# Graph attention kernel: the score vectors of the last two layers made in three column groups of TensorE's array

## The chip, the cores and the metric

The kernel runs on one core of one Trainium2 chip. The core has four engines that compute, each with its own instruction stream: TensorE (PE in the profile; its weight loads are listed as PEld), VectorE (DVE), ScalarE (ACT) and GpSimd (POOL). SyncE (SP) issues most DMAs here. The metric is the device time of one execution in microseconds (us), where lower is better.

## What is computed

The input is a graph of 1250 nodes with 768 features and 40000 edges of three types. There are four attention layers: two without relations (4 heads of 192, 2 heads of 96), then two with three relations (4 heads of 192, 1 head of 768). The part that the change touches is how the last two layers get their attention scores:

```python
def rgat_conv(x, W, q, k, b, src, dst, etype, heads, out_ch, n_nodes):
    xr = jnp.einsum('nd,rdf->rnf', x, W)        # W: 3 relations x 768 x 768
    oi = xr[etype, dst]
    oj = xr[etype, src]
    qi = oi @ q                                 # q, k: 768 x heads
    kj = oj @ k
    alpha = jax.nn.leaky_relu(qi + kj, NEG_SLOPE)
    m = jax.ops.segment_max(alpha, dst, num_segments=n_nodes)
    e = jnp.exp(alpha - m[dst])
    z = jax.ops.segment_sum(e, dst, num_segments=n_nodes)
    a = e / (z[dst] + EPS)
    msg = (a[:, :, None] * oj.reshape(-1, heads, out_ch)).reshape(-1, heads * out_ch)
    out = jax.ops.segment_sum(msg, dst, num_segments=n_nodes)
    return out + b
```

A node's score is x @ (W[r] @ q). So the kernel makes the small products W[r] @ q and W[r] @ k once, the score vectors: for each relation 768 numbers per head for q and as many for k. They depend on the weights alone, and are made early, long before the layer that uses them.

## The kernel before

The program is one hand-written instruction stream per engine, tied together by semaphores. The order on each engine is that of the code. Phases end with a barrier of all engines (`end_phase`). The first phase (0 to some 395 us) counts the edges into dense matrices, projects the first layer, and then has the mask stage, from 285 to 390 us of the span. Everything that the change moves is there.

The mask stage makes 40 masks (10 tiles of nodes x 4), each of which says where a row of the graph has no edge:

- DVE writes mask n in bf16 (`no_edges`, line 1683, into a ring of 3, so it waits until mask n-3 has been turned).
- PE turns it with 10 transposes (line 925) into PSUM bank 3 or 5; it waits for the mask (`nm_ready`) and until ACT has copied mask n-2 (`nm_copied`).
- ACT copies the turned mask to SBUF (line 1268, a ring of 6), and SP writes it to HBM (line 528, 320 KB).
- DVE, after every four masks, reads one of the turned masks four times, once for each head of the first layer (`tensor_tensor_reduce`, line 1697), to find the largest score of each node. Its results, the last of which ends the stage, give `pq`, which PE turns (line 935), ACT copies (line 1280) and SP sends through HBM. The first layer's attention waits for that.

Between the masks PE makes the score vectors. The weights come transposed in 12 halves (2 layers x 3 relations x 2 halves of 384 columns), each 1152 KB, into a ring of 3 in SBUF; POOL issues the load of half i when `score_rows` i-3 is done (line 722). After the masks 2, 5, 8 and so on PE runs `score_columns(i - 1)` and then `score_rows(i)`:

- `score_rows(i)` (line 902): six float32 matmuls, one for each 128 rows of the inner dimension f, added up in PSUM bank 7. The stationary operand is `qk1[:, f, :]` (8 columns: q and k of 4 heads) or `qk2[:, f, :]` (2 columns), the moving one is 128 x 384 of the weights. In the trace each float32 matmul is two rows, each with its own weight load.
- ACT copies the 8 or 2 result rows to `v_rows` (line 1259).
- `score_columns(i)` (line 910): three transposes of 128 columns each turn these rows into columns in bank 0; at the end ACT saves them in `vtab` (line 1278).

`cols` is a small table of constants, loaded by one DMA at the start, that holds `qk1` in its columns 24 to 71 and `qk2` in 72 to 83.

Of the kernel before, what the change touches and what calls it, by code (L numbers as in the profile page):

```python
# [20 lines left out]
F32 = mybir.dt.float32  # L21
# [4 lines left out]
ALU = mybir.AluOpType  # L26
ACT = mybir.ActivationFunctionType
AX = mybir.AxisListType

P = 128  # L30
N = 1250
D = 768
# [3 lines left out]
DT = D // P  # L36
# [67 lines left out]
C = Conv("c", [0, 1, 2], 4, 192, 384, 8, 4, 1, True, 1)  # L104
# [29 lines left out]
def gnn_program(nc, t_in, out):  # L134
    with ExitStack() as ctx:
        def sb(name, shape, dt):
            return ctx.enter_context(nc.sbuf_tensor(name, shape, dt))
# [21 lines left out]
        identf = sb("identf", [P, P], F32)  # L159
# [14 lines left out]
        epsc = sb("epsc", [P, 1], F32)  # L174
        winoff = sb("winoff", [P, NW], F32)
        tab = sb("tab", [1, 192], I32)
        cols = sb("cols", [P, 84], F32)
        scale2 = sb("scale2", [2, 1], F32)
        sconst = sb("sconst", [P, 4], F32)

        ps = ctx.enter_context(nc.psum_tensor("ps", [P, 8 * 512], F32))

        def bank(b, n=512, at=0):
            return ps[:, b * 512 + at:b * 512 + at + n]
# [16 lines left out]
        al2 = cols[0:96, 20:24].rearrange("p (j c) -> p j c", j=2)  # L201
        qk1 = cols[:, 24:72].rearrange("p (j c) -> p j c", j=DT)
        qk2 = cols[:, 72:84].rearrange("p (j c) -> p j c", j=DT)

# [45 lines left out]
        wt_half = [carve(work, i % 3 * WTH, WTH).rearrange("p (f d) -> p f d", f=DT) for i in range(12)]  # L252
        WT_HALVES = [(c, r, h) for c in (C, DD) for r in range(RELS) for h in range(2)]
# [3 lines left out]
        def v_cols(i, j):  # L257

            c, r, h = WT_HALVES[i]
            n2 = 2 * c.heads  # L260
            return (0 if c is C else RELS * DT * 8) + (r * DT + h * (DT // 2) + j) * n2
# [480 lines left out]
        def _(pe):  # L742
# [151 lines left out]
            def score_rows(i):  # L894

                c, r, h = WT_HALVES[i]
                pe.wait_ge(wt_in[i % 3], 16 * (i // 3 + 1))
                if i:
                    pe.wait_ge(v_copied, i)
                qk = qk1 if c is C else qk2  # L900
                for f in range(DT):
                    last = mm(ps[0:2 * c.heads, 7 * 512:7 * 512 + D // 2], qk[:, f, :], wt_half[i][:, f, :],
                              start=(f == 0), stop=(f == DT - 1))
                last.then_inc(v_done, 1)

            def score_columns(i):
                n2 = 2 * WT_HALVES[i][0].heads
                pe.wait_ge(v_copied, i + 1)
                for j in range(DT // 2):
                    last = nc.tensor.transpose(bank(0, n2, v_cols(i, j)),  # L910
                                               v_rows[i % 2][0:n2, j * P:(j + 1) * P], identf[0:n2, 0:n2])
                last.then_inc(v_turned, 1)


# [224 lines left out]
        def _(act):  # L1139
# [112 lines left out]
            nc.scalar.activation(s02[:, :, 0:A.RH], sd[:, :, 0:A.RH], ACT.Copy, scale=0.2)  # L1252

            def copy_v_rows(i):
                n2 = 2 * WT_HALVES[i][0].heads
                act.wait_ge(v_done, i + 1)
                if i >= 2:
                    act.wait_ge(v_turned, i - 1)
                nc.scalar.activation(v_rows[i % 2][0:n2, :], ps[0:n2, 7 * 512:7 * 512 + D // 2], ACT.Copy).then_inc(v_copied, 1)

            for n, (r, t) in enumerate(MASKS):
                act.wait_ge(nm_turned, n + 1)
# [251 lines left out]
        def _(dve):  # L1514
# [3 lines left out]
            def link(ins):  # L1518

                n_link[0] += 1  # L1520
                ins.then_inc(s_dve, 1)
                dve.wait_ge(s_dve, n_link[0])
# [61 lines left out]
            v.scalar_tensor_tensor(keyf[0:EC, :], tile_i[0:EC, :], float(W), keyf[0:EC, :], ALU.mult, ALU.add)  # L1584
            v.scalar_tensor_tensor(lof[0:EC, :], tile_i[0:EC, :], -float(P), src_i[0:EC, :], ALU.mult, ALU.add)
            link(v.scalar_tensor_tensor(nlof[0:EC, :], tile_i[0:EC, :], float(P), src_i[0:EC, :], ALU.mult, ALU.subtract))
            v.memset(brow[:, H2W:H2W + 1], 1.0).then_inc(keys_ready, 1)
            s = sems[A]

# [493 lines left out]
```

## Time and profile before

| | us |
|---|---|
| median of 3 executions | 1998.51 (1998.45 to 2000.24) |
| profiled execution, its time | 2000.49 |
| profiled execution, its span | 1998.7 |
| mask stage, from the first transposes to the last reduction | 285.5 to 390.1 |
| first `score_rows` to the transposes behind the last | 299.4 to 382.4 |
| PE busy, of the span | 1842.2 (92%) |
| DVE busy, of the span | 1489.9 (75%) |
| `score_rows` (line 902), 144 rows | 50.0 |
| `score_columns` (line 910), 36 rows | 4.2 |

Times in the trace count from the start of the span. A row of the timeline gives the start, the time from the first start to the last end of a run of equal instructions, and in brackets how long the engine had been idle before and what released it. A matmul's duration includes the time in which its result travels to PSUM; matmuls overlap, so the distance between starts is what one costs. PEclk is the granted share of TensorE's full clock.

### The profile page before, as it was taken

To read this page: it belongs to the slowest core of one execution; us is meant where nothing else is said; L and a number is where in the kernel's file an instruction comes from. 1 tells how busy PE (TensorE), PEld (TensorE's weight loads), DVE (VectorE), ACT (ScalarE), POOL (GpSimd) and SP (SyncE) were. 2 spreads that over 40 slices of the span, in tenths; PEclk is the share of its full clock that TensorE was granted. 3 is DMA by queue.
4 is the path that set the end of the run, shared out by engine and by line. 5 is a ranking of instruction groups with operands and counts; after the bars stand their busy time and mean duration, and the time that the engine had idled before them with its cause. 6 is when DMAs were issued, how large, how long until landed. Compare 5 with 4: busy or idle time off the path is not lost. (4 is left out here: it accounts for less than half of the span.)

```text
span 1998.7 us, 22525 instructions
## 1 busy us (share of the span) xinstructions
PE 1842.2 (92%) x7830; PEld 1275.1 (64%) x7831; DVE 1489.9 (75%) x2741; ACT 716.3 (36%) x1202; POOL 19.7 (1%) x38
## 2 busy tenths in 40 slices
PE   5789978679999899999699999998999979999997
PEld 3445544379944455555499999997655545555554
DVE  7869867789766663999699999995146027988996
ACT  5758965444213321111243434342311111322331
POOL 0000001010000000000000000000000000000000
PEclk9889999889999899999899999998999999999999
DMA  6200039652062316453322212112165437677764
GB/s 163 78 5 26 30 116 314 203 174 58 21 184 90 126 72 226 141 206 115 101 66 74 81 59 83 59 56 80 64 200 190 179 113 242 212 254 248 249 217 164
DMA packets 148943, 266.70 MB, mean 133 GB/s; under 512 B 11647, under 2 KB 118006, under 8 KB 145498
## 3 DMA queue, kind: packets, MB, share of 16 engines
q1 hardware_dynamic: 109002, 201.40, 30.6%
q10 hardware_dynamic: 36560, 49.66, 7.3%
q0 software_dynamic: 3264, 14.16, 2.5%
q8 instruction: 64, 1.05, 0.2%
q14 instruction: 53, 0.43, 0.1%
HBM read 209.46 MB, written 55.71 MB: 133 GB/s over the span
## 5 line engine op out<-in xcount | busy, mean ns | idle before, releaser
L1095 PE MATMUL ps<-work 128*128 128x193 f32 (+1 forms) x3200 | 531.0, 330 | 32.8 <-DVE work L1845 32.8
L1095 PEld LDWEIGHTS ps<-work 128*128 128x128 f32 x3200 | 530.4, 191 | 33.9 <-issue 33.9
L1045 PE MATMUL ps<-work 128*128 128x384 f32 (+2 forms) x1440 | 473.7, 490 | 5.7 <-ACT work L1303 2.6
L1045 PEld LDWEIGHTS ps<-work 128*128 128x128 f32 x1440 | 273.6, 191 | 197.1 <-issue 17.0
L1118 PE MATMUL ps<-work 128*128 128x384 f32 (+1 forms) x1050 | 341.2, 488 | 10.3 <-DVE work L1951 10.3
L1464 ACT ACTIVATE work<-work,s 128x1280 f32<-128x1280 f32 x160 | 218.0, 1363 | 293.4 <-DVE work L1839 293.3
L1118 PEld LDWEIGHTS ps<-work 128*128 128x128 f32 x1050 | 200.0, 191 | 151.5 <-issue 12.4
L1839 DVE SCALAR_TENSOR_TENSOR work<-work,sd 128x1280 f32<-128x1280 f32 x160 | 247.7, 1549 | 38.6 <-PE ps L1095 25.7
L1845 DVE SCALAR_TENSOR_TENSOR work<-work,counts 128x1280 f32<-128x1280 f32 x160 | 237.8, 1486 | 2.7 <-ACT work L1464 2.6
L1611 DVE TENSOR_SCALAR work<-work,winoff 125x480 bf16<-125x480 f16 x480 | 158.0, 401 | 0.1
L866 PE MATMUL ps<-work 125*128 125x480 bf16 x480 | 116.4, 393 | 33.3 <-ACT work L1208 16.2
L1484 ACT ACTIVATE work<-work,s 128x256 f32<-128x256 f32 x150 | 68.0, 500 | 220.6 <-DVE work L1924 220.5
L1402 ACT ACTIVATE work<-ps 128x384 f32<-128x384 f32 x90 | 44.3, 492 | 251.8 <-PE ps L1045 244.8
L866 PEld LDWEIGHTS ps<-work 125*128 125x128 bf16 x480 | 47.3, 102 | 97.7 <-issue 52.3
L1203 ACT ACTIVATE work<-work 125x128 f16<-125x128 f16 x320 | 102.1, 395 | 11.6 <-issue 9.8
L1786 DVE CUSTOM_DVE_ANT_0 feat<-feat,work 128x1280 bf16<-128x1280 f32 x50 | 74.5, 1491 | 30.4 <-DMA feat<-srow_d 28.5
L850 PE MATMUL ps<-feat,work 128*128 128x402 f32 (+1 forms) x240 | 84.9, 503 | 0.0
L1786 DVE CUSTOM_DVE_ANT_0 work<-feat,work 128x1280 bf16<-128x1280 f32 x50 | 74.5, 1491 | 6.9 <-DMA work<-nomask_d 6.9
L1770 DVE TENSOR_TENSOR counts<-counts 128x384 f32<-128x384 f32 x15 | 8.2, 557 | 91.6 <-ACT counts L1402 64.5
L850 PEld LDWEIGHTS ps<-feat,work 128*128 128x128 f32 x240 | 46.2, 193 | 32.2 <-issue 2.1
L1697 DVE CUSTOM_DVE_ANT_0 feat<-feat,work 128x1280 bf16<-128x1280 f32 x40 | 57.2, 1486 | 11.9 <-DMA feat<-srow_d 11.0
L1607 DVE TENSOR_SCALAR work<-work 125x128 bf16<-125x128 f16 x160 | 33.2, 251 | 41.6 <-PE ps L866 29.7
(220 smaller groups left out, 1539.6 us busy)
## 6 DMA issues: line engine op xcount, KB each, us to landing
work<-hs_d SPq DMA_DIRECT2D x75, 960.0 KB, 5.3
work<-pqrow_d SPq DMA_DIRECT2D x18, 1280.0 KB, 6.4
work<-nomask_d SPq DMA_DIRECT2D x70, 320.0 KB, 3.3
nomask_d<-work SPq DMA_DIRECT2D x40, 320.0 KB, 6.8
hx_d<-work ACTq DMA_DIRECT2D x60, 192.0 KB, 1.9
work<-hx_d SPq DMA_DIRECT2D x120, 96.0 KB, 1.9
hs_d<-counts ACTq DMA_DIRECT2D x45, 192.0 KB, 2.0
feat<-srow_d SPq DMA_DIRECT2D x3, 2560.0 KB, 12.5
```

Source lines behind the costliest of these rows:

```text
L850: last = mm(bank(5 + n % 2, A_COLS[p]), xT[:, j, t * P:(t + 1) * P], wg[p][:, j, :], start=(j == 0), stop=(j == DT - 1))
L866: return mm(bank(b, WROW), oh_lo[slot][0:EC, :], oh_hi[slot][0:EC, :], start=start, stop=False, skip_group_check=True)
L1045: last = mm(bank(n % 4 if i else n % 2, cols), xT[:, j, t * P:(t + 1) * P], wv[:, j, :], start=(j == 0), stop=(j == DT - 1))
L1095: last = mm(sums_at(c, t, u), xe[i % RING][:, t * P:(t + 1) * P], hx[:, i % RING, 0:1 + c.width], start=(r == 0 and k == 0 and t % TB == 0 ...
L1118: last = mm(bank(product_bank(g, i), width), a[:, at * P:(at + 1) * P], h[:, block_, 0:width], start=(m == 0), stop=(m == STEPS_D - 1), sk ...
L1203: last = nc.scalar.activation(lo_abs[0:EC, q * P:(q + 1) * P], iota_lo[0:EC, :], ACT.Abs, bias=nlof[0:EC, bass.ds(c0 + q, 1)])
L1464: nc.scalar.activation(xe[i % RING][:, 0:n_], xe[i % RING][:, 0:n_], ACT.Exp, bias=s02[:, k, bass.ds(rh, 1)], scale=0.8).then_inc(s.exp_do ...
L1484: nc.scalar.activation(w_, w_, ACT.Exp, bias=s02[:, p + q * TH, r:r + 1], scale=0.8).then_inc(d_exp, 1)
L1611: return v.tensor_scalar(oh_hi[slot][0:EC, :], iota_hi[0:EC, :], winoff[0:EC, bass.ds(w, 1)], keyf[0:EC, bass.ds(ch, 1)], ALU.add, ALU.is_ ...
L1786: v.tensor_tensor_reduce(junk(c, n * H + h), sbc_of(c, r)[:, h, :], nm_in(c, n), 1.0, -3.0e38, ALU.subtract, ALU.max, mx[:, t, r * H + h:r ...
L1839: v.scalar_tensor_tensor(xe[i % RING][:, 0:n_], pqb[slot][:, 0, lo:lo + n_], sd[:, k, bass.ds(rh, 1)], pqb[slot][:, 1, lo:lo + n_], ALU.ad ...
L1845: v.scalar_tensor_tensor(xe[i % RING][:, 0:n_], xe[i % RING][:, 0:n_], 3.0e38, counts[:, rel, k, lo:lo + n_], ALU.min, ALU.mult).then_inc( ...
```

## The change

Six matmuls with 8 or 2 stationary columns become six matmuls with 32 columns each, which are put in three column groups of the array: f = 0 and 3 at column 0, f = 1 and 4 at column 32, f = 2 and 5 at column 64. Each group has its own 32 partitions of bank 7, and holds a sum over two values of f. The 32 stationary columns are a slice of `cols` that begins at the wanted vectors; what stands behind them gives rows that nobody reads (`cols` grows from 84 to 114 columns so that the last slice fits). ACT copies 96 rows in place of 8 or 2. `score_columns` takes as stationary operand the 96 x 128 block of `v_rows`, and as moving operand `groups_sel`, a 96 x 8 matrix with ones at (c, c), (32 + c, c) and (64 + c, c): so one matmul turns the rows and adds up the three groups. It is a plain float32 matmul where it was a transpose. DVE builds `groups_sel` from the identity with two additions at the start.

```diff
-        cols = sb("cols", [P, 84], F32)
+        cols = sb("cols", [P, 114], F32)
+        groups_sel = sb("groups_sel", [96, 8], F32)
...
+        def vector_group(c, f):
+
+            at = 24 + 8 * f if c is C else 72 + 2 * f
+            return cols[:, at:at + 32]
...
-                qk = qk1 if c is C else qk2
+
                 for f in range(DT):
-                    last = mm(ps[0:2 * c.heads, 7 * 512:7 * 512 + D // 2], qk[:, f, :], wt_half[i][:, f, :],
-                              start=(f == 0), stop=(f == DT - 1))
+                    g = 32 * (f % 3)
+                    last = mm(ps[g:g + 32, 7 * 512:7 * 512 + D // 2], vector_group(c, f), wt_half[i][:, f, :],
+                              start=(f < 3), stop=(f >= 3), tile_position=(0, g), skip_group_check=True)
                 last.then_inc(v_done, 1)
 
             def score_columns(i):
                 n2 = 2 * WT_HALVES[i][0].heads
                 pe.wait_ge(v_copied, i + 1)
                 for j in range(DT // 2):
-                    last = nc.tensor.transpose(bank(0, n2, v_cols(i, j)),
-                                               v_rows[i % 2][0:n2, j * P:(j + 1) * P], identf[0:n2, 0:n2])
+                    last = mm(bank(0, n2, v_cols(i, j)), v_rows[i % 2][0:96, j * P:(j + 1) * P], groups_sel[:, 0:n2],
+                              start=True, stop=True, skip_group_check=True)
                 last.then_inc(v_turned, 1)
...
-                nc.scalar.activation(v_rows[i % 2][0:n2, :], ps[0:n2, 7 * 512:7 * 512 + D // 2], ACT.Copy).then_inc(v_copied, 1)
+                nc.scalar.activation(v_rows[i % 2][0:96, :], ps[0:96, 7 * 512:7 * 512 + D // 2], ACT.Copy).then_inc(v_copied, 1)
...
+            link(v.tensor_tensor(groups_sel[:, :], identf[0:96, 0:8], identf[0:96, 32:40], ALU.add))
+            link(v.tensor_tensor(groups_sel[:, :], groups_sel[:, :], identf[0:96, 64:72], ALU.add))
             v.memset(brow[:, H2W:H2W + 1], 1.0).then_inc(keys_ready, 1)
```

On PE the order of the work stays as it is. This is one round of the mask stage before, from `score_columns` of half 0 to the third mask behind it; a number is that of the row, then comes the line, then what is written and read, with partitions x columns of the moving operand for line 902 given as stationary columns x moving columns:

```order
371 L910 MATMUL ps<-identf,work 128x8 [waits v_copied]
372 L910 MATMUL ps<-identf,work 128x8 x2
373 L902 MATMUL ps<-work,cols 8x384 [waits v_copied,wt_in1]
374 L902 MATMUL ps<-work,cols 8x384 x5
375 L925 MATMUL ps<-identb,work 128x128 [waits nm_copied,nm_ready]
376 L925 MATMUL ps<-identb,work 128x128 x9
377 L925 MATMUL ps<-identb,work 128x128 [waits nm_copied,nm_ready]
378 L925 MATMUL ps<-identb,work 128x128 x9
```

And the same round of the changed kernel (its lines 909, 917 and 932 are 902, 910 and 925 of before):

```order
371 L917 MATMUL ps<-groups_sel,work 128x8 [waits v_copied]
372 L917 MATMUL ps<-groups_sel,work 128x8 x2
373 L909 MATMUL ps<-work,cols 32x384 [waits v_copied,wt_in1]
374 L909 MATMUL ps<-work,cols 32x384 x5
375 L932 MATMUL ps<-identb,work 128x128 [waits nm_copied,nm_ready]
376 L932 MATMUL ps<-identb,work 128x128 x9
377 L932 MATMUL ps<-identb,work 128x128 [waits nm_copied,nm_ready]
378 L932 MATMUL ps<-identb,work 128x128 x9
```

No matmul and no wait has moved: the six matmuls have 32 stationary columns for 8, and the three behind them read `groups_sel` for the identity.

On DVE, at the end of the setup of the edges, before the counting windows begin, this stands before:

```order
41 L1583 SCALAR_TENSOR_TENSOR work<-work 125x320 [waits s_dve]
42 L1584 SCALAR_TENSOR_TENSOR work<-work 125x320 [waits s_dve]
43 L1585 SCALAR_TENSOR_TENSOR work<-work 125x320
44 L1586 SCALAR_TENSOR_TENSOR work<-work 125x320
45 L1587 MEMSET brow 128x1 [waits s_dve]
```

and this in the changed kernel:

```order
42 L1590 SCALAR_TENSOR_TENSOR work<-work 125x320 [waits s_dve]
43 L1591 SCALAR_TENSOR_TENSOR work<-work 125x320
44 L1592 SCALAR_TENSOR_TENSOR work<-work 125x320
45 L1594 TENSOR_TENSOR groups_sel<-identf 96x8 [waits s_dve]
46 L1595 TENSOR_TENSOR groups_sel<-groups_sel,identf 96x8 [waits s_dve]
47 L1596 MEMSET brow 128x1 [waits s_dve]
```

The two additions stand ahead of the memset that tells the other engines that the keys are ready (`keys_ready`).

## Rows read from the trace of the kernel before

**Rows 1.** The page: span, and busy time of each engine.
```profile
span 1998.7 us, 22525 instructions
PE 1842.2 (92%) x7830; PEld 1275.1 (64%) x7831; DVE 1489.9 (75%) x2741; ACT 716.3 (36%) x1202; POOL 19.7 (1%) x38
```
**Rows 2.** Timeline of PE, mask stage: start, length, operation, idle before and releaser.
```profile
299.37 5.59 PE L902 MATMUL ps<-work,cols 128*8 128x384 f32 x12 [11.01 <-DMA work<-in_wt_c]
304.90 1.29 PE L925 MATMUL ps<-identb,work 128*128 128x128 bf16 x20
307.05 0.72 PE L925 MATMUL ps<-identb,work 128*128 128x128 bf16 x10 [0.86 <-ACT work L1268]
307.70 0.35 PE L910 MATMUL ps<-identf,work 8*128 8x8 f32 x3
307.98 4.04 PE L902 MATMUL ps<-work,cols 128*8 128x384 f32 x12
311.94 1.29 PE L925 MATMUL ps<-identb,work 128*128 128x128 bf16 x20
...
382.36 1.29 PE L925 MATMUL ps<-identb,work 128*128 128x128 bf16 x20
```
**Rows 3.** Line 902: durations in ns (least, median, most), first and last start.
```profile
L902 PEld LDWEIGHTS ps<-work,cols x144: 80/86/138, 299.4 to 381.6; 128*8 128x8 f32 x72, 128*2 128x2 f32 x72
L902 PE MATMUL ps<-work,cols x144: 484/486/847, 299.4 to 381.9; 128*8 128x384 f32 x72, 128*2 128x384 f32 x72
```
**Rows 4.** Timeline, weight loads inside line 902, at the lower and the higher clock.
```profile
301.26 0.14 PEld L902 LDWEIGHTS ps<-work,cols 128*8 128x8 f32 x1 [0.50 <-issue]
...
301.89 0.14 PEld L902 LDWEIGHTS ps<-work,cols 128*8 128x8 f32 x1 [0.50 <-issue]
...
308.63 0.09 PEld L902 LDWEIGHTS ps<-work,cols 128*8 128x8 f32 x1 [0.23 <-issue]
308.95 0.09 PEld L902 LDWEIGHTS ps<-work,cols 128*8 128x8 f32 x1 [0.23 <-issue]
```
**Rows 5.** Line 767: durations in ns, first and last start (a full-clock stretch).
```profile
L767 PEld LDWEIGHTS ps<-cols,feat x32: 163/165/166, 28.4 to 31.1; 96*96 96x96 f32 x32
L767 PE MATMUL ps<-cols,feat x32: 169/224/225, 28.6 to 31.2; 96*96 96x2 f32 x32
```
**Rows 6.** Timeline of DVE at the start of the program.
```profile
12.04 0.15 DVE L1566 TENSOR_TENSOR work<-work 80x1 f32<-80x1 f32 x1
12.23 0.15 DVE L1567 TENSOR_TENSOR work<-work 80x1 f32<-80x1 f32 x1
```
**Rows 7.** Timeline, end of the mask stage and what follows, all engines.
```profile
382.14 1.48 DVE L1683 TENSOR_SCALAR work<-counts 128x1280 bf16<-128x1280 uint16 x3
...
384.39 1.49 DVE L1697 CUSTOM_DVE_ANT_0 feat<-feat,work 128x1280 bf16<-128x1280 f32 x1 [0.78 <-ACT work L1268]
...
390.17 0.20 DVE L1794 TENSOR_TENSOR sd<-sd,sconst 128x40 f32<-128x40 f32 x1
...
391.90 2.29 PE L935 MATMUL ps<-identf,pq 128*8 128x128 f32 x10 [5.27 <-DVE pq L1810]
394.23 1.23 ACT L1280 ACTIVATE feat<-ps 8x1280 f32<-8x1280 f32 x1 [6.07 <-PE ps L935]
```
**Rows 8.** Timeline of DVE, the first reduction of the stage, and one later.
```profile
298.46 1.49 DVE L1697 CUSTOM_DVE_ANT_0 feat<-feat,work 128x1280 bf16<-128x1280 f32 x1 [11.00 <-DMA feat<-srow_d]
...
376.50 1.48 DVE L1697 CUSTOM_DVE_ANT_0 feat<-feat,work 128x1280 bf16<-128x1280 f32 x1
...
377.91 1.49 DVE L1697 CUSTOM_DVE_ANT_0 feat<-feat,work 128x1280 bf16<-128x1280 f32 x1
```
**Rows 9.** Stretches: PE, PEld, DVE, ACT, POOL busy (x), PEclk, DMA share, GB/s.
```profile
300.00:307.00 7.00, 6.19 (x32) 2.19 (x30) 5.71 (x9) 1.81 (x3) 0.83 (x1) 0.82 0.98 373
307.00:314.00 7.00, 6.19 (x45) 2.95 (x45) 6.20 (x10) 3.93 (x5) 0.83 (x1) 1.00 0.97 301
349.00:356.00 7.00, 6.18 (x45) 2.88 (x45) 7.00 (x12) 3.94 (x5) 0.94 (x1) 1.00 1.00 307
```
**Rows 10.** Waits in 285 to 395 us: who waited for what, us, times, longest.
```profile
PE ps L902 <- DMA work<-in_wt_c: 11.0, 1, 11.0
```
**Rows 11.** Stretches of 2 us, PE alone: busy (x), PEclk, DMA share, GB/s.
```profile
68.00:70.00 2.00, 0.93 (x5) 1.00 0.00 0
70.00:72.00 2.00, 0.41 (x2) 0.61 0.00 0
72.00:74.00 2.00, 2.00 (x7) 0.50 0.00 0
```

More of the change, by code:

```diff
@@ L1254, in copy_v_rows @@
             def copy_v_rows(i):
-                n2 = 2 * WT_HALVES[i][0].heads
                 act.wait_ge(v_done, i + 1)
@@ L2048 @@
     edges = lambda v: v.reshape(NCH, EC).T
-    cols = np.zeros((P, 84), np.float32)
+    cols = np.zeros((P, 114), np.float32)
     cols[:, 0:12:2] = a["L0_gnn_norm_b"].reshape(DT, P).T
```

## The prediction

> **What bounds the kernel now.** I read the page first [rows 1]: PE is busy for 92% of 1998.7 us, but that is an average over stages, and the change touches one stage of 105 us only. So the question is what ends that stage. The timeline of PE shows its round [rows 2]: three masks are turned, then come three column transposes and one `score_rows`. From 304.90 to 311.94 it lasts 7.04 us. Eleven such rounds lead from 304.90 to 382.36 (77.46 / 11 = 7.04), so none is longer for a special reason. A round consists of
>
> - 2.15 us from the first transposes to those of the third mask, 307.05; 0.86 of it is a wait for ACT's copy of an earlier mask;
> - 0.65 us for the third mask, up to 307.70;
> - 0.28 us for `score_columns`, up to 307.98;
> - 3.96 us for `score_rows`, up to 311.94. It is twelve rows whose weight loads start 0.32 us apart (308.63, 308.95) [rows 4], 12 x 0.323 = 3.88. Each row lasts 486 ns [rows 3], so some 0.163 us is travel that the next row hides.
>
> The end of the stage hangs on PE [rows 7]: the mask that DVE's last four reductions read is turned right behind the last `score_rows` (382.36), ACT has copied it at 384.39, the reductions run until 390.17, and the short chain over `pq` follows. What shortens PE's rounds moves 384.39 forward, and all that follows moves with it, since the next stage starts behind a barrier.
>
> DVE is next in line. A reduction costs 1.41 us from start to start (376.50, 377.91) [rows 8], a mask 1.48 / 3 = 0.49 [rows 7]. Four masks cost 4 x (1.41 + 0.49) = 7.6 us, thus 5.7 us for the three of a round. Its 40 reductions and 35 remaining masks from 298.46 on [rows 8] take 56.4 + 17.2 = 73.6 us, to 372.1. The stage can't end more than 18 us earlier, whatever PE does.
>
> **Part 1, `score_rows` in three groups.** No row of this trace has matmuls in different column groups, so the price is bounded from two sides. Upper end: nothing overlaps, twelve slots of 0.323 us, 3.88 as before. Lower end: all three groups run at once, 12 / 3 = 4 slots, 1.29 us. I take a value between, from the order of the rows. A float32 matmul is two rows, 144 rows for 72 matmuls [rows 3], and both rows of one matmul use the same group. If rows start in program order and a group takes one stream at a time, the second row of f = 0 waits for the first, and the first row of f = 1 starts together with it. Each matmul then shares only one of its slots with its neighbour: 6 + 1 = 7 slots, 7 x 0.323 = 2.26 us, which saves 1.62 us a round.
>
> The first `score_rows` runs at the lower clock. It lasts 5.53 us (299.37 to 304.90) [rows 2], with loads 0.63 to 0.64 apart at first (301.26, 301.89) [rows 4]. Seven slots, five at 0.64 and two at 0.323, are 3.85 us.
>
> The Trainium skill (TensorE: Matmul & The Clock Gate, part 3, on packing small matmuls) gives 2.38 times the speed for three column groups with 32 columns each and 512 moving ones. Applied here the rows would take about 3.88 / 2.38 = 1.6 us, an estimate by that page. No run here shows it. It is the second case below.
>
> **Part 2, going in and out of the groups.** The rows show no such change. Lower end 0. Upper end 1.0 us a round, twice the 0.486 us of a whole row [rows 3]. I take 0.4: twice the travel time of 0.163 that the next row no longer hides, plus one exposed weight load of 0.09 [rows 4]. The skill speaks here against the change: by TensorEngine Tiling (Array Packing), Key Properties, a change of the tiling mode drains TensorE. It gives no price, and no row shows one; with no drain the sum would be 0.4 a round lower.
>
> **Part 3, `score_columns`.** Three transposes become three float32 matmuls, six rows, each loading 128 columns of weights for 8 or 2 moving columns. The nearest row is line 767: 96 columns of weights for 2 moving columns, 32 rows in 2.81 us, 0.087 apart at the full clock [rows 5]. Six rows are 0.52 us if 128 columns cost the same, and 6 x 0.087 x 128/96 = 0.70 if they cost in proportion. Upper end: 165 ns, the duration of one such load [rows 5], six times, 0.99. I take 0.70, so +0.42 a round against 0.28 (0.24 to 0.71).
>
> **Part 4, the start.** DVE gets two small additions, each waiting for the one before it. Their like stand 0.19 us apart (12.04, 12.23) [rows 6]: +0.4 us, ahead of `keys_ready`, where all engines stand waiting, so nothing covers it. Lower end 0.
>
> **Parts at nothing.** ACT's copy of 96 rows for 8 has as many columns, and ACT is busy 3.93 of 7 us [rows 9]. The table grows by 30 columns in a DMA at the start that nobody waits for in the mask stage. The masks' loads and the stage behind `pq` are as before. DMA is the cover to watch: its share is 0.97 to 1.00 in most of the stage at 301 to 307 GB/s [rows 9]. A round moves 1152 + 3 x 320 KB, 2.16 MB, in 7.04 us. In 6.2 us that would be 348 GB/s. The stretch 300 to 307 moves 373 GB/s at a share of 0.98 [rows 9], so the share doesn't tell that the limit is reached. Except before the first half, PE waits for no weights [rows 10], and a load is issued three halves ahead.
>
> **The sum.** A round: -1.62 + 0.40 + 0.42 = -0.80, so 6.24 us; eleven of them -8.8. First `score_rows`: 5.53 to 3.85 + 0.4, -1.3. Start +0.4. One thing comes in new: four masks now cost PE 4/3 x 6.24 = 8.3 us, against DVE's 7.6, where they were 9.4. DVE works in blocks of 5.6 us of reductions in which it makes no mask, and its ring holds three. So now and then PE will wait for a mask. I take some +1.4 us in the whole stage (between 0 and 4; nothing in the rows has this rhythm). Together -8.8 - 1.3 + 0.4 + 1.4 = -8.3 us. The profiled execution took 2000.49 us, 1.8 more than its span and 2.0 more than the median, which is the better start: 1998.5 - 8.3 = **1990.2 us**.
>
> **The cases.**
>
> 1. *Half overlap*, as summed. With the changeover at 0 and the columns at their least it is -15, with the changeover at 1.0 it is -2: mostly 1985 to 1995. For it: two rows per matmul and a group that can't serve two at once. Chance 0.44.
> 2. *Full overlap*. Four slots, 1.29 us: a round falls by 2.59 - 0.82 = 1.77 to 5.3 us, under DVE's 5.7, and DVE becomes the bound. Eleven rounds save 11 x 1.34 = 14.7, the first `score_rows` 5.53 - 3.0 = 2.5 (four slots of 0.64 and 0.4), less 0.4 and some 1.8 for the uneven rhythm: -15, 1983.5 us. Against it: the two rows of a matmul need the same group. A value between both, as by the skill's page on the clock gate above, ends in about the same place, since DVE cuts it. Chance 0.24.
> 3. *No overlap, slower*. The twelve rows stream one after the other, for instance because all groups read the moving operand through one path. A round costs 7.04 + 0.40 + 0.42 = 7.86; eleven +9.0, the first +0.4, the start +0.4: +9.8, 2008.3 us; without a changeover +5, 2003.5. The change then doesn't do what it says. It decides where `score_rows` without changeover is over 3.96 - 0.82 = 3.1 us. For it: no row of this trace shows two matmuls streaming at once. Chance 0.19.
> 4. *DMA takes over*: if about 304 GB/s [rows 9] is all that this mix of transfers gives, a round stays at 2.16 MB / 304 GB/s = 7.1 us, and only the start and the first half change: about 1998 us. Against it is the 373 GB/s. With its partial forms, and case 1 with all costs at their ends, chance 0.08.
> 5. *The clock falls* inside the stage. From 68 to 72 us PE was busy for 1.3 of 4 us, and then stood at half clock for over 2 us [rows 11]. A round of the changed kernel still has no gap beyond one to two us. Rounds at half clock would last some 10 us, three of them +10: about 2005. Chance 0.05.
>
> **Numbers.** Likeliest is case 1, 1990.2. The range for 8 in 10 takes in cases 1, 2 and 4 and the lower part of 3: 1982 to 2006. About 4 us (0.2%) is what a measurement can tell from no change. Faster by more: cases 2 and nearly all of 1, 0.67. Within: 0.10. Slower: cases 3 and 5, 0.23.
>
> **What would show it.** In the timeline of PE the distance from the start of the six matmuls to the next transposes: 2.7 us if the overlap is half, 1.7 if full, 4.4 if none. The first starts inside it tell pairs from triples. The distance from the column matmuls to `score_rows`: 0.7, with 0.5 to 1.0 possible. The round: 6.2 us, and the row at 384.39 earlier by 8.7. DVE's waits for PE in the stage shrink, and PE's waits for DVE appear. The forecast is wrong if a DMA appears among the waits of `score_rows`, if PEclk is under 1.00 between 310 and 370, or if the stretch before 285 moves by other than 0.4 us.

## The result

| | kernel before | changed kernel |
|---|---|---|
| time, median (lowest to highest), us | 1998.48 (1997.89 to 2000.24) | 1978.03 (1975.89 to 1981.61) |
| ratio to before, 95% interval | 1 | 0.9898 (0.988 to 0.9916) |
| span of the profiled execution, us | 1998.7 | 1979.8 |
| mask stage, first reduction to the first operation behind the last, us | 298.46 to 390.17 = 91.7 | 301.69 to 377.06 = 75.4 |
| busy share of PE / DVE in the whole span | 92% / 75% [rows 1] | 92% / 75% |

The change made the kernel faster by 20.4 us. The forecast was 8.3 us faster with a range that ended at 1982.0, so the time lies below the range. Of the cases, the second is the one that came: full overlap, with DVE as the next bound.

The head of the page of the changed kernel, to be read against [rows 1]:

```profile
span 1979.8 us, 22599 instructions
PE 1818.9 (92%) x7866; PEld 1273.2 (64%) x7867; DVE 1487.6 (75%) x2743; ACT 717.1 (36%) x1202; POOL 19.4 (1%) x38
```

The timeline of PE in the changed kernel (start, duration, engine, line, operation, count, idle time before it and what ended it). `score_rows` is now line 909, `score_columns` 917, the turning of a mask 932. It answers to [rows 2]:

```profile
302.48 2.78 PE L909 MATMUL ps<-work,cols 128*32 128x384 f32 x12 [11.18 <-DMA work<-in_wt_c]
...
307.89 0.73 PE L932 MATMUL ps<-identb,work 128*128 128x128 bf16 x10 [0.39 <-DVE work L1692]
308.46 0.79 PE L917 MATMUL ps<-groups_sel,work 96*128 96x8 f32 x6
309.17 1.49 PE L909 MATMUL ps<-work,cols 128*32 128x384 f32 x12
310.60 1.29 PE L932 MATMUL ps<-identb,work 128*128 128x128 bf16 x20
312.75 0.72 PE L932 MATMUL ps<-identb,work 128*128 128x128 bf16 x10 [0.86 <-ACT work L1274]
313.30 0.79 PE L917 MATMUL ps<-groups_sel,work 96*128 96x8 f32 x6
314.02 1.49 PE L909 MATMUL ps<-work,cols 128*32 128x384 f32 x12
315.44 1.29 PE L932 MATMUL ps<-identb,work 128*128 128x128 bf16 x20
```

From the start of the twelve rows to the next transposes it is now 309.17 to 310.60, 1.43 us, where it was 3.96. From the column matmuls to `score_rows` it is 308.46 to 309.17, 0.71, where it was 0.28. A round whose only wait is the 0.86 us for ACT is 310.60 to 315.44, 4.84 us, against 7.04. DVE takes 7.4 us for four reductions and four masks (301.69 to 309.07 in its timeline), so 5.5 us for the three masks of a round (5.7 by the forecast's prices). PE's round is now the shorter one, and PE begins to wait for DVE, while DVE's waits for PE's turned masks fall from 17.5 to 4.1 us. The first line below is from the waits of the kernel before (285 to 395 us; who waited for what: us, times, longest), the next three from those of the changed kernel (280 to 395 us), the rest from PE's timeline:

```profile
DVE work L1683 <- PE ps L925: 17.5, 8, 4.4
```
```profile
DVE work L1692 <- PE ps L932: 4.1, 5, 2.2
PE ps L932 <- DVE work L1692: 10.3, 6, 2.8
PE ps L932 <- ACT work L1274: 6.9, 8, 0.9
```
```profile
323.05 1.29 PE L932 MATMUL ps<-identb,work 128*128 128x128 bf16 x20 [2.03 <-DVE work L1692]
...
324.97 2.78 PE L909 MATMUL ps<-work,cols 128*32 128x384 f32 x12
...
352.96 1.25 PE L932 MATMUL ps<-identb,work 128*128 128x128 bf16 x10 [2.82 <-DVE work L1692]
```

The stretches of 10 us, changed kernel (columns as in [rows 9]), show DVE busy for 9.5 to 10.0 of 10 us, and a granted clock under 1.00 in two of the four. DMA moves 402 to 411 GB/s at a share of 1.02 to 1.03 in the first three, and 353 GB/s at 0.90 in the last:

```profile
310.00:320.00 10.00, 8.28 (x105) 5.59 (x96) 9.79 (x17) 7.97 (x8) 1.66 (x2) 1.00 1.03 402
320.00:330.00 10.00, 7.15 (x74) 4.36 (x68) 9.97 (x17) 5.91 (x7) 1.65 (x2) 0.83 1.02 409
...
340.00:350.00 10.00, 7.84 (x96) 5.58 (x96) 9.97 (x17) 7.20 (x8) 1.59 (x2) 1.00 1.03 411
350.00:360.00 10.00, 6.89 (x51) 4.42 (x48) 9.46 (x15) 4.51 (x5) 0.06 (x1) 0.66 0.90 353
```

The ends of the stage in DVE's timeline, to be held against [rows 7] and [rows 8]:

```profile
301.69 1.49 DVE L1706 CUSTOM_DVE_ANT_0 feat<-feat,work 128x1280 bf16<-128x1280 f32 x1 [11.29 <-DMA feat<-srow_d]
...
377.06 0.20 DVE L1803 TENSOR_TENSOR sd<-sd,sconst 128x40 f32<-128x40 f32 x1
```

**The books of the stage.** These are the books of PE. With what the traces show in place of the forecast terms: eleven `score_rows` at 1.43 for 3.96 are -27.8 us; the columns, 0.71 for 0.28, +4.7; the third mask, 0.56 for 0.65, -1.0; the first `score_rows`, 2.71 for 5.53, -2.8. PE's waits for DVE are new, +10.3. Its waits for ACT fall from 11.6 to 6.9, -4.7. Rounds that ran at the half clock cost about 5.4: 1.0 in the transposes at 305.19, and 1.5 and 2.8 in the rounds that begin at 323.05 and 352.96. That is -27.8 + 4.7 - 1.0 - 2.8 + 10.3 - 4.7 + 5.4 = -15.9, against the -16.3 that the stage shows (75.4 - 91.7). Read from the starts alone: from the first `score_rows` to the transposes behind the last one PE took 83.0 us before (299.37 to 382.36) and takes 65.6 now (302.48 to 368.10), 17.4 less. From there to the stage's end it was 7.8 us and is 9.0, since this last piece now goes by DVE:

```profile
368.10 0.73 PE L932 MATMUL ps<-identb,work 128*128 128x128 bf16 x10
```

### The profile page after: what moved, and what is told of

It reads as the page before. It is cut to its first block and busy times, and to the rows that moved or that the text cites. A ratio compares the mean times of both kernels' runs of the same rounds, so it can differ in the third digit from the quotient of the medians.

```text
span 1979.8 us, 22599 instructions
## 1 busy us (share of the span) xinstructions
PE 1818.9 (92%) x7866; PEld 1273.2 (64%) x7867; DVE 1487.6 (75%) x2743; ACT 717.1 (36%) x1202; POOL 19.4 (1%) x38
## 5 line engine op out<-in xcount | busy, mean ns | idle before, releaser
L1052 PEld LDWEIGHTS ps<-work 128*128 128x128 f32 x1440 | 273.3, 191 | 197.5 <-issue 17.4
L1125 PE MATMUL ps<-work 128*128 128x384 f32 (+1 forms) x1050 | 341.3, 488 | 10.3 <-DVE work L1960 10.3
```

The source lines that it names most:

```text
L1052: last = mm(bank(n % 4 if i else n % 2, cols), xT[:, j, t * P:(t + 1) * P], wv[:, j, :], start=(j == 0), stop=(j == DT - 1))
L1125: last = mm(bank(product_bank(g, i), width), a[:, at * P:(at + 1) * P], h[:, block_, 0:width], start=(m == 0), stop=(m == STEPS_D - 1), sk ...
```

## The experiments

Each ratio is to the kernel before, run on the same chip, with a 95% interval. "The stage" is always the stretch of the table above. Line numbers of variants can be one to three higher than those of the changed kernel.

**One group.** All matmuls of `score_rows` in the first column group, the sum of six made in PSUM as before, but with the padded 32 columns, the column matmuls and the tiling:

```diff
-                    g = 32 * (f % 3)
+                    g = 0
...
-                              start=(f < 3), stop=(f >= 3), tile_position=(0, g), skip_group_check=True)
+                              start=(f == 0), stop=(f == DT - 1), tile_position=(0, g), skip_group_check=True)
...
-                    last = mm(bank(0, n2, v_cols(i, j)), v_rows[i % 2][0:96, j * P:(j + 1) * P], groups_sel[:, 0:n2],
+                    last = mm(bank(0, n2, v_cols(i, j)), v_rows[i % 2][0:32, j * P:(j + 1) * P], groups_sel[0:32, 0:n2],
```

> The changed kernel with all six matmuls in the column group at 0 (32 stationary columns, one sum over six f; the columns are made from 32 rows). Theory 'groups side by side': the gain of score_rows comes only from three groups that stream at once, so here twelve slots of 0.323 us follow one another, score_rows takes 3.96 us to the next transposes (1.42 in the changed kernel), a round is 7.4 us (2.15 + 0.55 + 0.72 + 3.96), and with no price for going in and out of a 32-column shape the kernel takes 1998.5 + 11 x 0.35 = 2002 us. Rival 'shape': the smaller shape of 32 columns streams faster by itself, score_rows is well under 3 us and the time stays near 1980. Rival 'changeover': going in and out costs 0.4 us a round, hidden so far by DVE as the bound: 4.4 us for score_rows, 2007 us.

Measured: 1999.39 us, ratio 1.0017 (1.0001 to 1.0034); stage 97.2 us. PE's timeline:

```profile
305.00 0.83 PE L917 MATMUL ps<-groups_sel,work 32*128 32x8 f32 x6
305.76 4.06 PE L909 MATMUL ps<-work,cols 128*32 128x384 f32 x12
309.75 1.29 PE L932 MATMUL ps<-identb,work 128*128 128x128 bf16 x20
```

The twelve rows take 3.99 us, as against 3.96 before. So going into the tiling and out of it costs 0.03 us together, and a tile of 32 columns streams no faster by itself (its rows, too, last 486 ns). The round is 7.55 us, longer by 0.51, nearly all of it the columns (0.76 for 0.28). The stage grew by 5.5 us, the time by only 3.4 (0.17% of 1997).

**Pairs.** Neighbouring matmuls in the same group, all three groups used:

```diff
-                    g = 32 * (f % 3)
+                    g = 32 * (f // 2)
...
-                              start=(f < 3), stop=(f >= 3), tile_position=(0, g), skip_group_check=True)
+                              start=(f % 2 == 0), stop=(f % 2 == 1), tile_position=(0, g), skip_group_check=True)
```

> The changed kernel with another order of the groups: f = 0, 1 at column 0, f = 2, 3 at 32, f = 4, 5 at 64, so that four rows in a row go to the same group. Theory 'a queue for each group': a group's rows wait only for rows of their own group, four slots as before, score_rows 1.42 us, 1978 us. Rival 'in order': a row waits until all before it have started; rows of neighbouring groups share one slot each, 12 - 2 = 10 slots, score_rows 3.3 us, a round of 6.7 us, some 1995 us (and in the changed kernel, whose three groups alternate by matmul, the same rule would have given 7 slots).

Measured: 1976.62 us, ratio 0.9895 (0.9877 to 0.9912); stage 75.5 us.

```profile
306.21 1.50 PE L909 MATMUL ps<-work,cols 128*32 128x384 f32 x12
307.65 1.29 PE L932 MATMUL ps<-identb,work 128*128 128x128 bf16 x20
```

The rows take 1.44 us, as in the changed kernel. In this order four rows of one group come one behind the other in the program, and that holds up nothing. The weight loads come in threes here too:

```profile
306.56 0.14 PEld L909 LDWEIGHTS ps<-work,cols 128*32 128x32 f32 x3 [0.19 <-issue]
```

The forecast's picture, that a matmul waits for its group while those behind it wait in line, doesn't hold. What sets the order in which the rows start instead is not shown.

**Two groups.** As one group, but `g = 32 * (f % 2)`, `start=(f < 2)`, `stop=(f >= DT - 2)`, and 64 rows copied and summed:

> The changed kernel with two column groups (f % 2), 64 rows copied and added. Theory 'groups side by side, DVE is now the bound': six slots, score_rows 2.07 us, an unhindered round of 5.5 us, still just under DVE's 5.7 for three masks and their reductions; so most of the gain stays: 1979 to 1982 us, with fewer and shorter waits of PE for DVE than the 10.3 us of three groups. Rival 'PE is still the bound': the 0.65 us more a round appear in full, 1978 + 11 x 0.65 = 1985 us.

Measured: 1982.13 us, ratio 0.9922 (0.9902 to 0.9942); stage 79.7 us.

```profile
306.09 2.13 PE L909 MATMUL ps<-work,cols 128*32 128x384 f32 x12
308.15 1.29 PE L932 MATMUL ps<-identb,work 128*128 128x128 bf16 x20
...
321.37 1.29 PE L932 MATMUL ps<-identb,work 128*128 128x128 bf16 x20 [1.25 <-DVE work L1692]
```

The rows take 2.06 us. With 3.99, 2.06 and 1.43 for one, two and three groups, the rows cost 12, 6 and 4 slots of 0.33 to 0.36 us: what counts is how many rows each group has. (Groups with unequal numbers of rows were not run.) The third group takes another 0.63 us from each round, 7 us in eleven, but the stage gives up only 4.3 (79.7 to 75.4). The times are 5.5 us apart in this set (1982.13, and 1976.62 for the pairs), between the 1 to 4 us of the theory and the 7 of the rival, and their intervals overlap; so it is the stage and the waits that speak, not the time. Here already the unhindered round, 5.62 us (308.15 to 313.77), is nearly as short as DVE's 5.5, and PE waits for DVE 7.6 us.

**Tables alone.** The kernel before with only the wider table of constants and DVE's two additions at the start:

```diff
-        cols = sb("cols", [P, 84], F32)
+        cols = sb("cols", [P, 114], F32)
+        groups_sel = sb("groups_sel", [96, 8], F32)
...
+            link(v.tensor_tensor(groups_sel[:, :], identf[0:96, 0:8], identf[0:96, 32:40], ALU.add))
+            link(v.tensor_tensor(groups_sel[:, :], groups_sel[:, :], identf[0:96, 64:72], ALU.add))
```

> The kernel before with nothing but the wider table (114 columns) and the two additions on DVE; TensorE's work is unchanged. Theory 'the mask stage gives all': +0.2 us at the start (18.05 to 18.25 in the traces), 1998.7 us, mask stage from the first reduction to the last 91.6 us as before. Rival 'layout': the 4 us that the changed kernel gained outside the mask stage (a broadcast that landed in 6.8 in place of 9.3 us in the second layer, and the clock behind it) come from tensors that lie elsewhere in memory: 1994 to 1996 us, with the same broadcast at some 6.8 us.

Measured: 1996.01 us, ratio 1.0001 (0.9985 to 1.0016); stage 92.2 us. The start costs nothing that can be timed. The whole gain comes from the other parts.

**The changed kernel again**, to see which differences of one trace come back:

> The changed kernel as it is, timed and profiled again beside the kernels of this set. The mask stage (first to last reduction) took 75.4 us in its first trace and 75.5 with the groups in pairs, against 91.7 and 92.2 in the two kernels without groups, so the stage gives 16.3 us. If the stage gives all, the time is 16 to 17 us below the kernel before; if something outside it comes with the change, 20 us as in the first comparison. The wait for the broadcast in the second layer is then 11.3 to 11.7 us again.

Measured: 1977.06 us, ratio 0.9903 (0.9876 to 0.993); stage 73.3 us, 2.1 us shorter than in its first trace. One trace gives the length of this stage to about 2 us. Where the 2 us are can be read. In the three traces of 75.4 to 75.5 us (the first one, the pairs and the third one below) two later rounds of PE run at half clock, and DVE waits once for some 2.2 us for a mask to be turned; in this one a single round does, and no wait of DVE inside the stage is over 0.6. This is the wait in the first trace:

```profile
364.03 0.49 DVE L1692 TENSOR_SCALAR work<-counts 128x1280 bf16<-128x1280 uint16 x1 [2.21 <-PE ps L932]
```

**Three heads.** The fourth head's reduction is left out, to take 14 us of work from DVE:

```diff
+                    if h == 3:
+                        v.memset(mx[:, t, 3:4], 0.0).then_inc(s.max_done.sem, 1)
+                        continue
```

> The changed kernel without the reductions of the fourth head in the mask stage (a memset in their place, so the fourth head's scores are bounded by another number; that part of the computation is left out). Theory 'DVE is the bound of the changed stage': 10 x 1.41 = 14 us less on DVE, which then has 30 x 1.41 + 35 x 0.43 = 57 us; PE's own rounds of 4.84 us come to the front: 3.5 + 11 x 4.84 + 2 + 3 x 1.41 = 63 us for the stage where it is 75.4, and PE's waits for DVE (10.3 us) all but vanish. Rival 'PE or DMA is the bound': the stage stays within 3 us of 75.

Measured: 1975.29 us in a single execution; stage 70.3 us (298.79 to 369.06), where 63 was expected if PE alone were next. One stretch of 20 us, ACT's waits for the masks to be written out, and one wait of DVE:

```profile
320.00:340.00 20.00, 15.57 (x183) 10.45 (x182) 18.32 (x34) 15.65 (x16) 3.56 (x4) 1.00 1.03 413
...
ACT work L1274 <- DMA nomask_d<-work: 6.6, 9, 1.2
...
358.57 0.49 DVE L1692 TENSOR_SCALAR work<-counts 128x1280 bf16<-128x1280 uint16 x1 [4.37 <-PE ps L932]
```

The stage gave 3 to 5 us for 14 us less work, so neither the theory (12 us) nor the rival (within 3 us of 75) came out. DVE is the first bound, but not by much. Behind it stand, close together, PE and ACT's wait for the masks to be written out, with DMA at 413 GB/s. DVE itself waited for PE in turn: 11.2 us in all.

**Masks ahead.** DVE makes its masks one tile earlier, with a ring of six in place of three, so that PE need not wait through a block of reductions:

```diff
-MASK_RING, MASKS_OUT = 3, 6
+MASK_RING, MASKS_OUT = 6, 6
...
-            no_edges(0)
+            for n in range(5):
+                no_edges(n)
...
-                for n in range(4 * t + 1, min(4 * t + 5, 4 * T)):
+                for n in range(4 * t + 5, min(4 * t + 9, 4 * T)):
```

> The changed kernel with six mask buffers for three, and DVE four masks further ahead: masks 5 to 8 are made while it waits for the scores' broadcast, before the first reduction. Theory 'DVE is the bound, 3.6 us of its stage are waits for PE': the stage shrinks from 75.4 to 40 x 1.41 + 31 x 0.43 = 69.8 us and what waits are left, 70 to 72: 4 to 5 us below the changed kernel. Rival 'PE, ACT or DMA comes in': DVE's waits for PE grow instead, and less than 2 us are won.

Measured: 1977.74 us, ratio 0.9903 (0.988 to 0.9927); stage 72.8 us. PE's waits for DVE fell from 10.3 to 2.1 us, and in their place stand 11.7 us of waits for ACT (6.9 before this edit). The stage is 0.4 to 2.6 us shorter than in the two traces above, not the 4 to 5 of the theory, and the time is the same as that of the changed kernel (1977.06 in this set). DVE's own work is 69.7 us here (40 reductions, 31 masks), and 2.6 of the other 3.1 are waits for PE, most of it one wait near the start:

```profile
308.20 0.73 DVE L1692 TENSOR_SCALAR work<-counts 128x1280 bf16<-128x1280 uint16 x1 [2.21 <-PE ps L932]
```

**Masks ahead and rows later.** In addition PE's `score_rows` and ACT's copy come one round later:

```diff
-                if n % 3 == 2 and n // 3 < 12:
-                    if n // 3:
-                        score_columns(n // 3 - 1)
-                    score_rows(n // 3)
+                if n % 3 == 2 and n > 2:
+                    if n > 5:
+                        score_columns(n // 3 - 2)
+                    score_rows(n // 3 - 1)
```

> As the one before, and score_rows begins three masks later (behind masks 5, 8 and so on), so that PE turns masks 3 to 5 while the first weights are still on their way (it waits 11.2 us for them). Theory: DVE's first waits for PE go too, the stage is at 69.8 to 70.5 us, 5 us below the changed kernel and at most 1 us below the one before this. Rival: the last score_rows now stands ahead of mask 39 alone, which no reduction needs, but PE's idle time moves and its clock falls inside the stage: no gain, or up to 2 us lost, against the one before.

Measured: 1973.23 us, ratio 0.9875 (0.9847 to 0.9902); stage 69.7 us. PE's timeline shows masks turned while the first weights are on their way:

```profile
294.04 0.72 PE L932 MATMUL ps<-identb,work 128*128 128x128 bf16 x10 [0.41 <-ACT work L1274]
303.00 2.78 PE L909 MATMUL ps<-work,cols 128*32 128x384 f32 x12 [8.24 <-DMA work<-in_wt_c]
```

The wait for the weights is 8.24 us where it was 11.18. From 310 to 370 us DVE is busy for all of the 60 us (56.6 in the changed kernel, 49.6 in the kernel before). Now the stage is as long as DVE's own work.

**The last two side by side.** The changed kernel and the version above once more, in one set:

> The changed kernel once more, with more rounds, to settle how much of the gain lies outside the mask stage. In the traces the stage gives 16.3 to 18.4 us. Theory 'the stage gives all': ratio to the kernel before 0.991 to 0.992, 16 to 18 us. Rival 'something outside comes with it': 0.9895 to 0.990, 20 to 21 us, as in the three comparisons so far of kernels with three groups (0.9898, 0.9903, 0.9895).

> The kernel with masks made ahead and score_rows three masks later, timed again with more rounds. Its stage took 69.7 us where the changed kernel's took 73.3 and 75.4. Theory: 4 to 6 us faster than the changed kernel in the same set. Rival: its first profile had a late start of the stage (302.5 for 298.7) and the gain is lost there: within 2 us.

Measured: the changed kernel 1975.16 us, 0.9892 (0.9875 to 0.991), stage 75.5; masks ahead and rows later 1974.37 us, 0.9884 (0.9866 to 0.9903), stage 70.0. The stage is 5.5 us shorter, the time by 0.8 us, and the intervals overlap. In the other set the two differed by 3.8 us (1977.06 and 1973.23). The shorter stage is shown twice; that the kernel as a whole is faster is not.

**The same edits on the kernel before.** Masks ahead and rows later, with no column groups:

> The kernel before (one group of 8 or 2 columns, transposes) with only the other two edits of the best version: six mask buffers with masks made ahead, and score_rows three masks later. Theory 'PE bounds the stage before': DVE's lead is worth nothing, but PE turns three masks (2.8 us) while the weights are on their way, and the last score_rows (3.96 + the third mask's 2 us) leaves the path of the last reduction: 6 to 8 us below the kernel before, the stage 84 to 86 us for 91.7. Rival 'the two edits only matter where DVE is the bound': within 2 us of before.

Measured: 1989.2 us, ratio 0.9957 (0.9942 to 0.9972), 8.6 us faster; stage 85.3 us. That is what the theory had, so the two edits are worth something where PE is the bound, too. But the two changes go to the same place: by their ratios they give 19 to 22 and 8.6 us alone, and together 23 to 25, not 28 to 30.

**The kernel before again:**

> The kernel before, profiled again. Its first trace has 14.0 us of waiting for the broadcast in the second layer and half clock behind it, all later traces 11.3 to 11.7 us and full clock. Theory 'chance': about 11.5 us here too, and a span some 5 us shorter outside the mask stage. Rival 'it belongs to the kernel before': 14 us again.

Measured: 1999.2 us; stage 92.95 us. The wait for the broadcast in the second layer, 13.99 us in the first trace of before, is 11.73 here; in the changed kernel it is this:

```profile
548.26 1.49 DVE L1795 CUSTOM_DVE_ANT_0 feat<-work 128x1280 bf16<-128x1280 f32 x1 [11.66 <-DMA work<-srow_d]
```

The 18.9 us between the first two spans can so be told by place. The stage is 16.3 shorter. It starts 3.2 later (301.69 for 298.46), though in this trace of the kernel before it starts at 301.92 and in the last one of the changed kernel at 295.69. All that lies behind the last reduction is 5.8 shorter (1998.7 - 390.2 = 1608.5, and 1979.8 - 377.1 = 1602.7). But there the first trace of the kernel before stands alone: its second trace has 1602.5, and the one group, which is no faster, 1599.8 (1992.8 - 393.0). Neither the 3.2 nor most of the 5.8 comes with the change.

## Why the prediction was right or wrong

**What bounds the kernel.** Right. PE's work in this stage was the bound before. With `score_rows` at 3.99 us and all else new, nothing was gained.

**Part 1, the failed step.** "Each matmul then shares only one of its slots with its neighbour: 6 + 1 = 7 slots." Measured were 4 slots, 1.43 us, near the lower end of 1.29, where 2.26 were forecast. The first `score_rows` likewise took 2.71 us for 4.25 (3.85 + 0.4). The step argued from an order in which a second row of a group blocks those behind it. The pairs show that no such order rules: by the same reasoning they would need 4 + 3 + 3 = 10 slots, and they took 1.44 us. The weight loads of the changed kernel come in threes, as many as there are groups, 0.32 us apart, where before single ones stood 0.32 us apart [rows 4]:

```profile
309.17 0.15 PEld L909 LDWEIGHTS ps<-work,cols 128*32 128x32 f32 x6
309.52 0.12 PEld L909 LDWEIGHTS ps<-work,cols 128*32 128x32 f32 x3 [0.20 <-issue]
309.84 0.12 PEld L909 LDWEIGHTS ps<-work,cols 128*32 128x32 f32 x3 [0.20 <-issue]
```

Rows are no shorter for it: each still lasts 486 ns at the full clock, the same as in [rows 3].

```profile
L909 PE MATMUL ps<-work,cols x144: 486/486/848, 302.5 to 367.7; 128*32 128x384 f32 x144
```

I had a lower end of 1.29 us and gave it a chance of 0.24. Half overlap rested on reasoning, with no row behind it, and should have had no more weight than full overlap. The Trainium skill (TensorE: Matmul & The Clock Gate, part 3) gives 2.38 times for three groups. The 1.6 us estimated from it was far nearer to the measured 1.43 than the 2.26 of the sum, and about as near as the lower end of 1.29; the trace shows 3.96 / 1.43 = 2.8 times.

**Part 2, the changeover.** Wrong by 0.37 us a round: 0.03 in place of 0.40 (one group). Eleven times this is 4 us, all on the side of too slow. The Trainium skill (TensorEngine Tiling (Array Packing), Key Properties) has a change of tiling mode drain the array; no cost of that is seen here beyond the 0.03.

**Part 3, the columns.** Right: 0.71 us measured for 0.70. Six rows in 0.71 are 0.118 apart, against 0.087 with 96 columns in line 767 [rows 5]; the ratio, 1.36, is near the 128/96 that was taken. With only 32 partitions in place of 96 it was 0.76 (one group).

**Part 4, the start.** Right. From the last operation ahead of the two additions to the memset behind them it was 0.55 us before (16.61 to 17.16) and is 0.94 (16.44 to 17.38): +0.39, where 0.4 was expected. The tables alone made a ratio of 1.0001, so it can't be seen in the time.

**The turn in rhythm.** The mechanism was right, PE waiting for masks through a block of reductions, and its size was off: 10.3 us in place of 1.4. The 1.4 was for a round of 6.24 us, 0.5 above DVE's. At 4.84 us PE must lose the whole difference. The experiment with masks ahead took 8 of the 10.3 us away, and the time stayed: 4.8 us came back as waits for ACT. So these waits are mostly how DVE's bound shows itself, and no separate cost.

**DVE's floor.** "The stage can't end more than 18 us earlier" was a little too near. The mask was put at 0.49, a third of the 1.48 us of three masks, the last of which had started late. Four in a row go from 307.34 to 309.07, 0.43 each, in the changed kernel:

```profile
307.34 1.81 DVE L1692 TENSOR_SCALAR work<-counts 128x1280 bf16<-128x1280 uint16 x4
309.07 1.48 DVE L1706 CUSTOM_DVE_ANT_0 feat<-feat,work 128x1280 bf16<-128x1280 f32 x1
```

With 0.43 the floor is 56.4 + 35 x 0.43 = 71.5 us. The stage took 73.3 to 75.5 in the traces of this kernel. In both traces with masks ahead and rows later it took 69.7 and 70.0; there four masks more are made ahead of the first reduction, and the floor is 56.4 + 31 x 0.43 = 69.7.

**The cases.** Case 2 forecast 1983.5 and -15; the time was 1978.0. The stage itself came to -16.3, so the mechanism and its size held, and the other 4 us lie elsewhere. Four traces of the changed kernel and of the pairs average 74.9 us in the stage, three of the kernel before or with its tables 92.3: -17.4 us. The timed gains of the four are 19.4 to 21.6. The difference, 2 to 4 us, was not found. (17.4 us would be a ratio of 0.9913, inside or within 0.0003 of each of the four intervals.) What lies outside the stage is 1896.5 to 1904.4 us in the four (1972.0 - 75.5, 1979.8 - 75.4) and 1900.3 to 1907.0 in the three (1992.5 - 92.2, 1998.7 - 91.7); with masks ahead and rows later it is 1906.6 and 1902.3, and with one group, which gains nothing, 1895.6. So single traces of this program scatter by some 10 us outside the stage, and whether a part of it belongs to the change stays open. Case 1's price of -8.3 fell with part 1. Case 3 was refuted by one group: without overlap the same edits cost 3.4 us. In case 4, 304 GB/s would have been the limit of DMA; the changed kernel's trace shows up to 411. The 373 GB/s of [rows 9] was the row to go by. In case 5, "a round of the changed kernel still has no gap beyond one to two us" was wrong: PE waited up to 2.8 us, and the rows at 324.97 and 355.32 ran at half clock, 2.78 us each. It cost less than the case's 10 us. By the books it is 5.4 us of PE's time, part of which PE would have spent waiting for DVE; the trace with one such round fewer, and without DVE's wait of 2.2 us, has a stage 2.1 us shorter.

**The signs.** Those of the changed round came: DVE's waits for PE shrank, PE's for DVE appeared, and the last four reductions began 13.1 us earlier (371.30 for 384.39) where 8.7 was forecast. Of the three signs of being wrong, no DMA appeared among the waits of `score_rows` but the one ahead of the first. The granted clock did fall under 1.00 between 310 and 370 us. And the stretch before 285 moved by 2.9 us (the first transposes at 285.49 before, at 288.43 now), which was no effect of the change: it is 289.01 in the second trace of the kernel before and 285.50 in the second of the changed one.

**The range** ended at 1982.0 because case 2's price, 1983.5, was nearly its lower end. The case's own uncertainty should have been added: a floor that is 2 us lower, and several us by which the time and the stage differ. With these, as is easily said afterwards, it would have reached to about 1978.

## What to carry to other kernels

Where PE is the bound and streams many rows for few output columns, splitting their sum over column groups can pay, as it did here. Count the rows of each group, add the cost of summing the groups (0.43 us a round here), and put the changeover near nothing (0.03 here). Then ask how far the next engine is from its own floor: of the 26.9 us that PE's own work lost here, 10.3 came back as waits for DVE. Where a case's mechanism caps the gain, take the cap from starts, not from durations, and let the range reach beyond it.

## What the runs showed of the hardware

- Three column groups of 32 columns with 128 x 384 moving float32 values ran truly side by side: 12 rows in 3.99, 2.06 and 1.43 us in one, two and three groups, with each row at 486 ns throughout. The order in which the groups are named in the program made no difference (1.43 and 1.44).
- DMA's busy share was no measure of what is left. It stood at 0.97 to 1.00 with 301 to 307 GB/s [rows 9], and at 1.02 to 1.03 with 402 to 413 GB/s in the changed kernel and with three heads.
- PE's clock was halved inside the stage behind waits of 2.03 and 2.82 us (the rows at 323.05 and 352.96 above), though PE was busy for 7 of the 10 us around. Another wait of 2.04 us did not bring it down, and the next `score_rows` took 1.49 us, as PE's timeline of the changed kernel shows in the first two rows below. In the second trace of the same kernel it is the other way round (the last three rows): the row behind a wait of 2.81 us ran at full clock, 0.73 us for ten transposes, and the half clock came behind a wait of 2.04. So the length of a wait alone doesn't tell.

```profile
345.58 1.29 PE L932 MATMUL ps<-identb,work 128*128 128x128 bf16 x20 [2.04 <-DVE work L1692]
...
347.42 1.49 PE L909 MATMUL ps<-work,cols 128*32 128x384 f32 x12
```
```profile
327.48 0.73 PE L932 MATMUL ps<-identb,work 128*128 128x128 bf16 x10 [2.81 <-DVE work L1692]
...
342.64 1.55 PE L932 MATMUL ps<-identb,work 128*128 128x128 bf16 x20 [2.04 <-DVE work L1692]
...
345.30 2.78 PE L909 MATMUL ps<-work,cols 128*32 128x384 f32 x12
```
